# q·k as three fp32r products in row tiles of 32, in place of six bf16 products in row tiles of 64

## The chip, the cores and the metric

One core of one Trainium2 chip. The metric is the device time of one execution in microseconds (us).

## What is computed

The reference, cut to what matters here (4 batches of 1024 tokens, width 128, 16 heads of width 8, 8 experts of which a router weighs the best two for each token):

```python
xn  = layernorm(x)                                   # (4, 1024, 128), fp32
zn  = layernorm(xn) * ln_w + ln_b
q, k, v = split(zn @ W_qkv + b_qkv)                  # each (4, 16, 1024, 8)
scores = einsum('bhqd,bhkd->bhqk', q, k) / sqrt(8)   # the products that the change is about
attn = softmax(scores);  msa = attn @ v
s = xn + msa @ W_proj + b_proj
ffn = sum over e of weight[e] * (gelu(xn @ W1[e] + b1[e]) @ W2[e] + b2[e])
result = x + s * silu(ffn)
```

## The kernel before

The results must be nearly as exact as fp32. Matmuls get there in three ways: fp32 operands as they are (each then has two records in the profile), operands split into two fp32r parts and multiplied in three products (most of the experts), and, for q and k, operands split into three bf16 parts and multiplied in six products.

**The rows of q and k.** The 4096 tokens are worked through in 8 groups g of 512. For each, q and k (w = 0 and 1) come transposed into `qk_full`. VectorE casts them to the first bf16 part (`first`, L1153), GpSimd subtracts that part (`rest`, L547), VectorE casts the second (`second`, L1159), and GpSimd makes the third (`third`, L554). These four steps stand in slots 20 to 26 of a group's 32. SyncE then stores the parts in HBM (`sp_store_qk`, L398 to L405) so that each of a head's 8 dimensions has six slots, with the parts of q and of k in such an order that slot times slot gives the six products. A head so has 48 rows, and one matmul with 48 contraction rows sums all six products over all dimensions. In the stacks for the scores three more rows hold the negative maximum of each query: 51 rows.

**Two heads at a time.** There are 32 pairs p of heads. A pair is loaded (`sp_rows`, L424) into slot p % 2 of a stack: its first head at partitions 0 and up, its second at 64 and up (`HALF`). Matmuls whose rows lie in different halves run side by side in TensorE's array, those in the same half one after the other. `q_max_stack` and `k_max_stack` serve the maxima (L867), `q_stack` and `k_stack` the scores that are exponentiated (L927).

**The expert phase** takes the first 523 us or so. TensorE goes through 32 slots for each group, most with three fp32r matmuls up (L832, L833, L834) and three down (L853, L854, L856; each fourth one is in fp32, L848). Beside them, 128 early maximum steps (`early_scores`, at `EARLY_AT`) cover head pairs 0 to 7: each is two matmuls of L867, one for each head, which VectorE reduces in one instruction (L1237). GpSimd and VectorE split the experts' hidden values (`h_lo`, L612 and L1181), and SyncE's queue, worked off in program order, loads each group's tokens `xz` (L381), for which VectorE's L1079 waits.

**The attention phase** has 256 blocks n of 128 keys of a pair p = n // 8. Each has two halves of 512 queries. A half is two matmuls of L927 (one for each head), which fill one of two PSUM buffers, and one ACTIVATE of 128x1024 on ScalarE (L753), the exponential. Beside the scores of blocks 0 to 239 TensorE computes the maxima of later pairs (L867, pairs 8 to 31), 3.2 matmuls a block, each into one of three PSUM banks and reduced by its own VectorE instruction (L1219); their pair is p' = 8 + n // 10. The order on TensorE in a half is: scores of one head, maximum of the other head, scores of the other head, and mostly a maximum of the first. The scores of a half wait until the exponential of the half before the last is done. After a block's two halves come the 8 records (4 matmuls) of attn @ v (L947) of the block before the last, and now and then transposes (L901 of the maxima, L960 of the output). Engines wait for each other by semaphores, and every engine works in program order.

Of the kernel before, what the change touches and what calls it, by code (L numbers as in the profile page):

```python
# [5 lines left out]
ALU = mybir.AluOpType  # L6
# [7 lines left out]
P = 128  # L14
TG = 512
TT = TG // P
PARTS = 3
SLOTS = 6
Q_PARTS = (0, 1, 2, 0, 1, 0)
K_PARTS = (0, 1, 0, 1, 0, 2)  # L20
HALF = 64
# [33 lines left out]
def attention_and_experts(nc, x, ln_w, ln_b, w_qkv, b_qkv, w_proj, b_proj, w1, b1, w2, b2, w_r, b_r, out):  # L55
# [25 lines left out]
    assert D == P and N % TG == 0 and N // TG == 2 and HID % P == 0 and SROWS <= HALF  # L81
# [5 lines left out]

    q_dram = nc.dram_tensor("q_rows_dram", (B, D, SLOTS, N), BF16, kind="Internal").ap()
    k_dram = nc.dram_tensor("k_rows_dram", (B, D, SLOTS, N), BF16, kind="Internal").ap()
    w_dram = nc.dram_tensor("expert_w_dram", (NG, TT, E, P), F32, kind="Internal").ap()  # L90
    m_dram = nc.dram_tensor("neg_max_dram", (PAIRS, NM, P), BF16, kind="Internal").ap()

    with ExitStack() as ctx:
# [11 lines left out]
        q_s = sb("q_stack", [P, 2, N], BF16)  # L105
        k_s = sb("k_stack", [P, 2, N], BF16)
        q_m = sb("q_max_stack", [P, 2, N], BF16)
        k_m = sb("k_max_stack", [P, 2, N], BF16)
        ident = sb("ident", [P, P])
        ident_b = sb("ident_b", [P, P], BF16)  # L110
# [3 lines left out]
        nmp = sb("neg_max_parts", [P, 2, 2, PARTS, NT], BF16)  # L114
        nmT = sb("neg_max_t", [NM, 2, P], BF16)
# [19 lines left out]
        qkp = fs("qk_parts", [P, 2, PARTS, TG], BF16)  # L135
# [162 lines left out]

        def split(i):

            return i % HC < SC
# [61 lines left out]
        QP_ST = 6 * 16  # L363
# [25 lines left out]
        def sp_store_qk(sp, g):  # L389
# [13 lines left out]
            sp.dma_start(dst[:, 0:2, :], qkp[:, 1, 0:2, :]).then_inc(S("qp_st"), 16)  # L403
            sp.dma_start(dst[:, 2:4, :], qkp[:, 1, 0:2, :]).then_inc(S("qp_st"), 16)
            sp.dma_start(dst[:, 4:6, :], qkp[:, 1, 0:3:2, :]).then_inc(S("qp_st"), 16)  # L405
# [25 lines left out]
        def sp_load_max(sp, p):  # L431
# [3 lines left out]
            for hh in range(2):  # L435
                sp.dma_start(q_s[HALF * hh + QROWS:HALF * hh + SROWS, slot, :],
# [920 lines left out]
```

## Time and profile before

| | us |
|---|---|
| median of three runs (1129.59 to 1134.57) | 1129.85 |
| the profiled execution's own time | 1131.14 |
| its span, from first to last instruction | 1129.3 |

| engine | busy us | share of the span |
|---|---|---|
| TensorE matmuls | 1062.4 | 94% |
| TensorE weight loads | 438.8 | 39% |
| VectorE | 896.3 | 79% |
| ScalarE | 847.7 | 75% |
| GpSimd | 365.0 | 32% |

A matmul's record lasts from its start until its result has drained, so that records of matmuls that follow each other overlap: the distance of two starts says how long a matmul holds the array, not the duration of its record. The mean granted TensorE clock was 0.988 of full speed.

### The profile page before, as it was taken

The page shows a single profiled execution, that of the slowest core. Times are in us where ns is not written, and L with a number is a line of the kernel's source. Part 1 is how long each engine was busy: PE and PEld are TensorE (multiplying, and loading weights), DVE is VectorE, ACT ScalarE, POOL GpSimd, SP SyncE. Part 2 cuts the span into 40 slices and gives each one's busy share as a digit, 9 for nine tenths or more (in the row PEclk, how much of TensorE's full clock was granted, in tenths as well). Part 3 has the DMA queues.
Part 4 walks back from the last instruction along what each step waited for, and adds up shares of the span by engine and source line. Part 5 has one row for each costly group of instructions (what it writes and reads, how often), then busy time and mean ns, then how long its engine had stood idle before and what let it go on. Part 6 is the DMA issues. An engine that isn't in the chain of part 4 may idle for free.

```text
span 1129.3 us, 17260 instructions
## 1 busy us (share of the span) xinstructions
PE 1062.4 (94%) x6041; PEld 438.8 (39%) x6041; DVE 896.3 (79%) x1567; ACT 847.7 (75%) x1133; POOL 365.0 (32%) x534
## 2 busy tenths in 40 slices
PE   5698999999999999999999999999999999999995
PEld 4475656566666666663122222222121212212123
DVE  7566778777768687666999999999999999999715
ACT  6575666566666666667988898888889898988982
POOL 3795656656666666453010001000000000000001
PEclk9899999999999999998999999999999999999998
DMA  4523131414141322223111112111211111111102
GB/s 144 150 83 84 61 86 29 117 34 118 32 114 33 102 51 64 75 72 92 45 44 44 39 35 56 32 45 29 58 31 44 40 48 45 30 44 30 30 1 75
DMA packets 84992, 67.42 MB, mean 60 GB/s; under 512 B 9277, under 2 KB 71402, under 8 KB 84906
## 3 DMA queue, kind: packets, MB, share of 16 engines
q1 hardware_dynamic: 84906, 66.32, 21.7%
q8 instruction: 48, 0.79, 0.3%
q14 instruction: 38, 0.31, 0.1%
HBM read 51.08 MB, written 15.20 MB: 59 GB/s over the span
## 4 chain that ended last, share of the span: by engine, by line
PE 53%; ACT 19%; DVE 6%; issue 4%; ACTq 0%; DVEq 0%; POOL 0%; POOLq 0%
ACT p_ring L753 17%; PE psum L947 13%; PE psum L927 11%; PE psum L867 6%; PE psum L832 4%; PE psum L848 3%; PE psum L834 3%; PE psum L833 3%; PE psum L856 2%; PE psum L853 2%; PE psum L854 2%; DVE neg_max_half L1237 2%; PE psum L960 2%; DVE neg_max_half L1219 1%; PE psum L981 1%
## 5 line engine op out<-in xcount | busy, mean ns | idle before, releaser
L753 ACT ACTIVATE p_ring<-psum 128x1024 f32<-128x1024 f32 x512 | 500.7, 1023 | 66.0 <-PE psum L927 62.3
L1219 DVE TENSOR_REDUCE neg_max_half<-psum 128x1 f32<-128x512 f32 x768 | 486.3, 684 | 38.1 <-PE psum L867 29.0
L867 PE MATMUL psum<-k_max_stack,q_max_stack 48*128 48x512 bf16 x1024 | 300.6, 386 | 15.7 <-DVE neg_max_half L1237 9.6
L927 PE MATMUL psum<-q_stack,k_stack 51*128 51x512 bf16 x1024 | 279.1, 383 | 12.9 <-ACT p_ring L753 3.7
L947 PE MATMUL psum<-p_ring,v_sb 128*9 128x512 f32 x2048 | 268.5, 597 | 0.4 <-ACT o_sb L744 0.4
L716 ACT ACTIVATE h_hi<-psum,cols 128x512 fp32r<-128x512 f32 x192 | 132.0, 688 | 152.1 <-PE psum L834 147.9
L612 POOL TENSOR_TENSOR h_lo<-h_split,h_hi 128x512 fp32r<-128x512 f32 x128 | 164.5, 1289 | 141.0 <-ACT h_split L719 139.2
L1237 DVE TENSOR_REDUCE neg_max_half<-psum 128x2 f32<-128x1024 f32 x128 | 156.5, 1222 | 60.6 <-PE psum L867 60.4
L927 PEld LDWEIGHTS psum<-q_stack,k_stack 51*128 51x128 bf16 x1024 | 60.3, 94 | 305.8 <-ACT p_ring L753 281.4
L568 POOL CAST neg_max_parts<-neg_max_rest 128x16 bf16<-128x16 f32 x32 | 6.7, 211 | 510.6 <-DVE neg_max_rest L1228 510.6
L719 ACT ACTIVATE h_split<-psum,cols 128x512 f32<-128x512 f32 x192 | 130.9, 682 | 0.0
L832 PE MATMUL psum<-xn_t_hi,w_hi 128*128 128x512 f32 x256 | 128.4, 502 | 1.2 <-DVE w_lo L292 1.2
L867 PEld LDWEIGHTS psum<-k_max_stack,q_max_stack 48*128 48x128 bf16 x1024 | 69.6, 93 | 116.6 <-issue 43.3
L834 PE MATMUL psum<-xn_t_lo,w_hi 128*128 128x512 f32 x256 | 102.1, 399 | 0.0
L833 PE MATMUL psum<-xn_t_hi,w_lo 128*128 128x512 f32 x256 | 101.7, 397 | 0.0
L1181 DVE TENSOR_TENSOR h_lo<-h_split,h_hi 128x512 fp32r<-128x512 f32 x64 | 53.7, 839 | 50.8 <-ACT h_split L719 50.8
L856 PE MATMUL psum<-h_lo,w_hi 128*128 128x512 f32 x192 | 77.2, 402 | 9.1 <-POOL h_lo L612 4.6
L853 PE MATMUL psum<-h_hi,w_hi 128*128 128x512 f32 x192 | 76.4, 398 | 0.0
L854 PE MATMUL psum<-h_hi,w_lo 128*128 128x512 f32 x192 | 76.0, 396 | 0.0
L603 POOL TENSOR_TENSOR acc<-acc,prod 128x512 f32<-128x512 f32 x48 | 65.8, 1371 | 15.0 <-DVE prod L1198 15.0
L947 PEld LDWEIGHTS psum<-p_ring,v_sb 128*9 128x9 f32 x2048 | 31.0, 88 | 92.4 <-issue 92.1
L848 PE MATMUL psum<-h_full,w_full 128*128 128x512 f32 x128 | 65.4, 592 | 0.0
(114 smaller groups left out, 920.4 us busy)
## 6 DMA issues: line engine op xcount, KB each, us to landing
expert_w_bc<-expert_w_dram SPq DMA_DIRECT2D x64, 256.0 KB, 4.9
k_rows_dram<-qk_parts SPq DMA_DIRECT2D x24, 256.0 KB, 3.0
q_max_stack<-q_rows_dram SPq DMA_DIRECT2D x64, 96.0 KB, 2.5
k_max_stack<-k_rows_dram SPq DMA_DIRECT2D x64, 96.0 KB, 2.5
q_stack<-q_rows_dram SPq DMA_DIRECT2D x64, 96.0 KB, 2.5
k_stack<-k_rows_dram SPq DMA_DIRECT2D x64, 96.0 KB, 2.5
q_rows_dram<-qk_parts SPq DMA_DIRECT2D x8, 384.0 KB, 2.6
xz<-in_L_attn_z_dram SPq DMA_DIRECT2D x8, 256.0 KB, 3.2
```

The lines of the kernel that those rows point to most:

```text
L612: pool.tensor_tensor(hl[:, (g * HS + j) % HR, :], h32[:, (g * HS + j) % FR, :], hh[:, (g * HS + j) % HR, :].bitcast(F32), ALU.subtract)\
L716: act.activation(hh[:, (g * HS + j) % HR, :], up, ACT.Gelu, bias=col(C_B1 + i))\
L719: act.activation(h32[:, (g * HS + j) % FR, :], up, ACT.Gelu, bias=col(C_B1 + i))\
L753: act.activation(p_sb[:, n % PR, a, :, :].rearrange("p h t -> p (h t)"), scores_bank[s % 2], ACT.Exp, scale=SCALE).then_inc(S("P"), 1)
L832: pe.matmul(o, w1h[:, e, ws], G(xh, g), start=True, stop=False)
L833: pe.matmul(o, w1l[:, e, ws], G(xh, g), start=False, stop=False)
L834: pe.matmul(o, w1h[:, e, ws], G(xl, g), start=False, stop=True).then_inc(S("h"), 1)
L867: return pe.matmul(to, q_m[rows, slot, t * P:(t + 1) * P], k_m[rows, slot, c * TG:(c + 1) * TG], start=True, stop=True)
L927: i = pe.matmul(scores_bank[s % 2][:, hh * TG:(hh + 1) * TG], k_s[rows, slot, kt * P:(kt + 1) * P], q_s[rows, slot, a * TG:(a + 1) * TG], ...
L947: i = pe.matmul(o_bank[at:at + VR, :], v_sb[:, b * KT + kt, 2 * (p % PB) + hh, :], p_sb[:, n % PR, a, hh, :], start=(kt == 0), stop=(kt == ...
L1219: dve.tensor_reduce(mx[:, p % MXR, c, hh * NT + t:hh * NT + t + 1], ring_bank(("max", u)), AX.X, ALU.max, negate=True).then_inc(S("R"), 1)
L1237: dve.tensor_reduce(mx[:, p % MXR, c, :].rearrange("p (h t) -> p h t", h=2)[:, :, t], early_bank, AX.X, ALU.max, negate=True).then_inc(S(" ...
```

## The change

q and k are split into two fp32r parts (`PARTS` = 2), whose three products fill three slots (`SLOTS` = 3): a head has 24 rows, 26 with the parts of its maximum. Each head takes a row tile of 32 partitions: pairs with even p the tiles at partitions 0 and 32, pairs with odd p those at 64 and 96, so that the stacks need no second slot. VectorE's second cast is gone, and GpSimd makes the second part in one step. Of the maximum's parts GpSimd makes two in two steps, not three in four. The stores are four instead of six for a group. The numbers of matmuls, reductions and exponentials stay the same.

```diff
-PARTS = 3
-SLOTS = 6
-HALF = 64
+PARTS = 2
+SLOTS = 3
+ROWS = 32
...
-        q_s = sb("q_stack", [P, 2, N], BF16)
-        k_s = sb("k_stack", [P, 2, N], BF16)
+        q_s = sb("q_stack", [P, N])
+        k_s = sb("k_stack", [P, N])
...
+        def tile_row(p, hh):
+
+            return ROWS * (2 * (p % 2) + hh)
...
-            sp.dma_start(dst[:, 0:3, :], qkp[:, 0, :, :]).then_inc(S("qp_st"), 16)
-            sp.dma_start(dst[:, 3:5, :], qkp[:, 0, 0:2, :]).then_inc(S("qp_st"), 16)
-            sp.dma_start(dst[:, 5:6, :], qkp[:, 0, 0:1, :]).then_inc(S("qp_st"), 16)
+            sp.dma_start(dst[:, 0:2, :], qkp[:, 0, :, :].bitcast(F32)).then_inc(S("qp_st"), 16)
+            sp.dma_start(dst[:, 2:3, :], qkp[:, 0, 0:1, :].bitcast(F32)).then_inc(S("qp_st"), 16)
...
-                        pool.tensor_tensor(qkf[:, w, :], qkf[:, w, :], qkp[:, w, 0, :], ALU.subtract)\
-                            .then_inc(S("r1"), 1)
-                    return step
-
-                def third(w):
-                    def step():
-                        wait(pool, "p1", g, 2, w + 1)
-                        pool.tensor_tensor(qkp[:, w, 2, :], qkf[:, w, :], qkp[:, w, 1, :], ALU.subtract)\
+                        pool.tensor_tensor(qkp[:, w, 1, :], qkf[:, w, :], qkp[:, w, 0, :].bitcast(F32), ALU.subtract)\
                             .then_inc(S("qp"), 1)
...
-                slot = p % 2
-                rows = slice(HALF * hh, HALF * hh + QROWS)
-                return pe.matmul(to, q_m[rows, slot, t * P:(t + 1) * P], k_m[rows, slot, c * TG:(c + 1) * TG],
+                rows = slice(tile_row(p, hh), tile_row(p, hh) + QROWS)
+                return pe.matmul(to, q_m[rows, t * P:(t + 1) * P].bitcast(F32R),
+                                 k_m[rows, c * TG:(c + 1) * TG].bitcast(F32R),
                                  start=True, stop=True)
...
-                def second(w):
-                    def step():
-                        wait(dve, "r1", g, 2, w + 1)
-                        dve.tensor_copy(qkp[:, w, 1, :], qkf[:, w, :]).then_inc(S("p1"), 1)
-                    return step
...
-                        20: [first(0)], 21: [first(1)], 24: [second(0)], 25: [second(1)], 28: [values]}
+                        20: [first(0)], 21: [first(1)], 28: [values]}
```

TensorE's program keeps its order. On GpSimd, this stood at the splitting of group 1 before (L547 and L554 split q and k, L612 splits the experts' hidden values, L603 adds up the experts):

```order
L547 TENSOR_TENSOR qk_full<-qk_full,qk_parts 128x512
L612 TENSOR_TENSOR h_lo<-h_split,h_hi 128x512
L603 TENSOR_TENSOR acc<-acc,prod 128x512
L554 TENSOR_TENSOR qk_parts<-qk_full,qk_parts 128x512
L612 TENSOR_TENSOR h_lo<-h_split,h_hi 128x512
L554 TENSOR_TENSOR qk_parts<-qk_full,qk_parts 128x512
```

And this stands there now, from the same place on (its L547, L600 and L591 are the former L554, L612 and L603):

```order
L547 TENSOR_TENSOR qk_parts<-qk_full,qk_parts 128x512
L600 TENSOR_TENSOR h_lo<-h_split,h_hi 128x512
L591 TENSOR_TENSOR acc<-acc,prod 128x512
L600 TENSOR_TENSOR h_lo<-h_split,h_hi 128x512 x2
L591 TENSOR_TENSOR acc<-acc,prod 128x512
```

The parts of k are complete two instructions of GpSimd's own splitting earlier, ahead of one addition and one or two steps of the experts. Behind them SyncE stores the parts, loads the stacks of pairs 0 and 1 and then `xz`.

## Rows read from the trace of the kernel before

**Rows 1.** Busy us (xcount) of each engine in stretches, clock, DMA:

```profile
200.00:300.00 100.00, 94.94 (x399) 60.50 (x397) 75.49 (x128) 60.88 (x105) 63.17 (x95) 1.00 0.30 78
832.87:923.92 91.05, 88.57 (x636) 18.60 (x632) 84.19 (x148) 80.73 (x91) 3.31 (x16) 1.00 0.15 41
923.92:1014.97 91.05, 88.57 (x636) 18.61 (x632) 84.20 (x148) 80.73 (x91) 3.31 (x16) 1.00 0.15 41
```

**Rows 2.** Groups by form: busy us, mean ns of one, idle before:

```profile
L753 ACT ACTIVATE p_ring<-psum 128x1024 f32<-128x1024 f32 x512 | 500.7, 1023 | 66.0 <-PE psum L927 62.3
L1219 DVE TENSOR_REDUCE neg_max_half<-psum 128x1 f32<-128x512 f32 x768 | 486.3, 684 | 38.1 <-PE psum L867 29.0
L1237 DVE TENSOR_REDUCE neg_max_half<-psum 128x2 f32<-128x1024 f32 x128 | 156.5, 1222 | 60.6 <-PE psum L867 60.4
```

**Rows 3.** Timeline, expert phase: start us, duration us; matmuls, then weight loads:

```profile
299.61 0.40 PE L856 MATMUL psum<-h_lo,w_hi 128*128 128x512 f32 x1
299.94 0.39 PE L867 MATMUL psum<-k_max_stack,q_max_stack 48*128 48x512 bf16 x2
300.26 0.50 PE L832 MATMUL psum<-xn_t_hi,w_hi 128*128 128x512 f32 x1
300.60 0.39 PE L833 MATMUL psum<-xn_t_hi,w_lo 128*128 128x512 f32 x1
300.83 0.39 PE L834 MATMUL psum<-xn_t_lo,w_hi 128*128 128x512 f32 x1
...
299.94 0.10 PEld L867 LDWEIGHTS psum<-k_max_stack,q_max_stack 48*128 48x128 bf16 x2 [0.36 <-issue]
300.26 0.19 PEld L832 LDWEIGHTS psum<-xn_t_hi,w_hi 128*128 128x128 f32 x1 [0.23 <-issue]
300.37 0.19 PEld L833 LDWEIGHTS psum<-xn_t_hi,w_lo 128*128 128x128 f32 x1
```

**Rows 4.** Timeline, attention phase: exponentials, matmuls, weight loads:

```profile
844.26 3.88 ACT L753 ACTIVATE p_ring<-psum 128x1024 f32<-128x1024 f32 x4 [0.98 <-PE psum L927]
848.47 1.02 ACT L753 ACTIVATE p_ring<-psum 128x1024 f32<-128x1024 f32 x1 [0.33 <-PE psum L927]
...
846.79 1.04 PE L947 MATMUL psum<-p_ring,v_sb 128*9 128x512 f32 x8
847.77 0.39 PE L927 MATMUL psum<-q_stack,k_stack 51*128 51x512 bf16 x1
848.00 0.59 PE L927 MATMUL psum<-q_stack,k_stack 51*128 51x512 bf16 x2
...
846.25 0.09 PEld L927 LDWEIGHTS psum<-q_stack,k_stack 51*128 51x128 bf16 x1 [0.63 <-ACT p_ring L753]
847.76 0.09 PEld L927 LDWEIGHTS psum<-q_stack,k_stack 51*128 51x128 bf16 x1 [0.86 <-ACT p_ring L753]
847.77 0.11 PEld L867 LDWEIGHTS psum<-k_max_stack,q_max_stack 48*128 48x128 bf16 x2
847.78 0.10 PEld L927 LDWEIGHTS psum<-q_stack,k_stack 51*128 51x128 bf16 x1
```

**Rows 5.** Timeline, last blocks, which have no maxima beside them:

```profile
1083.99 0.39 PE L927 MATMUL psum<-q_stack,k_stack 51*128 51x512 bf16 x2 [0.27 <-ACT p_ring L753]
1084.31 1.04 PE L947 MATMUL psum<-p_ring,v_sb 128*9 128x512 f32 x8
...
1086.13 5.75 ACT L753 ACTIVATE p_ring<-psum 128x1024 f32<-128x1024 f32 x6
```

**Rows 6.** Timeline, group 1's parts of k and group 2's tokens:

```profile
69.38 1.34 POOL L547 TENSOR_TENSOR qk_full<-qk_full,qk_parts 128x512 f32<-128x512 f32 x1
76.19 1.17 POOL L554 TENSOR_TENSOR qk_parts<-qk_full,qk_parts 128x512 bf16<-128x512 f32 x1
77.38 0.54 SPq L403 DMA_DIRECT2D k_rows_dram<-qk_parts  x1
86.02 0.42 SPq L381 DMA_DIRECT2D xz<-in_L_attn_z_dram  x1
...
89.29 0.29 DVE L1079 BATCH_NORM_STATS2 bn_parts<-xz 128x6 f32<-128x128 f32 x1 [7.80 <-DMA xz<-in_L_attn_z_dram]
...
90.23 0.50 PE L856 MATMUL psum<-h_lo,w_hi 128*128 128x512 f32 x1 [2.55 <-DVE h_lo L1181]
92.33 0.63 PE L854 MATMUL psum<-h_hi,w_lo 128*128 128x512 f32 x1
```

More of the change, by code:

```diff
@@ L80, in attention_and_experts @@
     NM = 2 * PARTS * NT
[L81 removed]
+    assert D == P and N % TG == 0 and N // TG == 2 and HID % P == 0 and SROWS <= ROWS
     x_g = x.rearrange("b (g t p) d -> (b g) p t d", p=P, t=TT)
     out_g = out.rearrange("b (g t p) d -> (b g) p t d", p=P, t=TT)
[L88 to L89 removed]
+    q_dram = nc.dram_tensor("q_rows_dram", (B, D, SLOTS, N), F32, kind="Internal").ap()
+    k_dram = nc.dram_tensor("k_rows_dram", (B, D, SLOTS, N), F32, kind="Internal").ap()
     w_dram = nc.dram_tensor("expert_w_dram", (NG, TT, E, P), F32, kind="Internal").ap()
[L91 removed]
+    m_dram = nc.dram_tensor("neg_max_dram", (PAIRS, NM, P), F32, kind="Internal").ap()
     with ExitStack() as ctx:
@@ L535, in _ @@
         def _(pool):
-            for n, t in enumerate((ident, ident_b)):
-                pool.memset(t[:, :], 0.0).then_inc(S("pool"), 1)
-                pool.wait_ge(S("pool"), n + 1)
-                pool.affine_select(out=t[:, :], in_=t[:, :], compare_op=ALU.not_equal, fill=1.0, base=0,
-                                   pattern=[[-1, P]], channel_multiplier=1).then_inc(S("ident"), 1)
+            pool.memset(ident[:, :], 0.0).then_inc(S("pool"), 1)
+            pool.wait_ge(S("pool"), 1)
+            pool.affine_select(out=ident[:, :], in_=ident[:, :], compare_op=ALU.not_equal, fill=1.0, base=0,
+                               pattern=[[-1, P]], channel_multiplier=1).then_inc(S("ident"), 1)
             ch = Chain(pool, S("pool_own"))
@@ L622, in padding @@
             def padding():
-                pool.memset(k_s[:, :, :], 1.0).then_inc(S("ones"), 1)
+                pool.memset(k_s[:, :], 1.0).then_inc(S("ones"), 1)
                 pool.memset(v_sb[:, :, :, DH:VR], 1.0).then_inc(S("v_ones"), 1)
@@ L724, in neg_max_t @@
             def neg_max_t(p, early=False):
-                m_tr = (b5 if early else ring_bank(("mT", p)))[0:NM, 0:P // 2].bitcast(BF16)
+                m_tr = (b5 if early else ring_bank(("mT", p)))[0:NM, 0:P]
                 act.wait_ge(S("mT"), p + 1)
@@ L767, in _ @@
         def _(pe):
-            pe.wait_ge(S("ident"), 2)
+            pe.wait_ge(S("ident"), 1)
             pe.wait_ge(S("rows"), 6 * 16)
@@ L899, in m_t @@
                     ring_free(pe, ("mT", p))
-                m_tr = (b5 if early else ring_bank(("mT", p)))[0:NM, 0:P // 2].bitcast(BF16)
-                pe.transpose(m_tr, nmp[:, p % 2, :, :, :].rearrange("p h i t -> p (h i t)"), ident_b[:, :])\
+                m_tr = (b5 if early else ring_bank(("mT", p)))[0:NM, 0:P]
+                pe.transpose(m_tr, nmp[:, p % 2, :, :, :].rearrange("p h i t -> p (h i t)").bitcast(F32), ident[:, :])\
                     .then_inc(S("mT"), 1)
@@ L925, in scores @@
                 for k, hh in enumerate((first, 1 - first)):
-                    rows = slice(HALF * hh, HALF * hh + SROWS)
-                    i = pe.matmul(scores_bank[s % 2][:, hh * TG:(hh + 1) * TG], k_s[rows, slot, kt * P:(kt + 1) * P],
-                                  q_s[rows, slot, a * TG:(a + 1) * TG], start=True, stop=True)
+                    rows = slice(tile_row(p, hh), tile_row(p, hh) + SROWS)
+                    i = pe.matmul(scores_bank[s % 2][:, hh * TG:(hh + 1) * TG], k_s[rows, kt * P:(kt + 1) * P].bitcast(F32R),
+                                  q_s[rows, a * TG:(a + 1) * TG].bitcast(F32R), start=True, stop=True)
                     if k:
```

35 lines of the change are left out of this document (14 added, 21 removed).

## The prediction

> **What bounds the kernel now.** I read the busy times by stretch first. In the expert phase TensorE is busy for 94.94 of 100 us and every other engine for at most 75.49 [rows 1], so what TensorE's program gains or loses there, the kernel does. In the attention phase the stretches repeat exactly: 91.05 us each, with 636 matmul records [rows 1]. A block has 8 + 4 + 3.2 = 15.2 records, and 40 blocks with their 28 transposes make 636, so a stretch is 40 blocks and a block takes 2.28 us. VectorE is busy for 84.19/40 = 2.10 us of it and ScalarE for 80.73/40 = 2.02 us. None of the engines is full: they wait for each other. The groups say the same, with 66.0 us in which ScalarE idles before its exponentials, nearly all for L927, and 38.1 us in which VectorE idles before its single reductions [rows 2].
>
> The timeline shows the loop that sets the pace of an undisturbed stretch. Four exponentials start at 844.26, the next at 848.47, 0.33 us after ScalarE fell idle [rows 4]: 4.21 us for two blocks. Two exponentials of that stretch must end before the scores whose weights load at 846.25 may start. From there TensorE is without a break on the path: scores and maxima, attn @ v at 846.79, scores again at 847.77, the second head's at 848.00, whose end frees the exponential at 848.47 [rows 4]. The remaining 0.17 us a block (2.28 less 2.11) comes from transposes and from maxima that wait for a PSUM bank. So half of the loop is TensorE's, and its matmuls count in both phases.
>
> **What the change costs on TensorE.** The rate of streaming hardly changes. Full-array fp32r matmuls start 0.23 us apart (300.60 to 300.83) [rows 3], and bf16 score pairs 847.77 to 848.00, also 0.23 [rows 4]. I take 0.01 us more for each step of two.
>
> The weights are dearer. A bf16 load of 128 columns lasts 0.10 us, an fp32r one 0.19, and the next fp32r load starts 0.11 us after it (300.26, 300.37) [rows 3]. Behind running matmuls that is hidden: L833 starts at 300.60, long after its load, and its record lasts the usual 0.39. Where the array changes its tiling, it isn't: L832 behind the maximum pair lasts 0.50 instead of 0.39, and its successor starts 0.34 us later instead of 0.23. The bf16 pair at the same kind of place lasts 0.39 with its load exposed [rows 3]. An exposed fp32r load thus costs 0.10 us more than a bf16 one. No row shows fp32r weights in a row tile; the bounds are 0 (the load hides in the change of tiling) and 0.19 (the whole record). I take 0.10, since the fp32r row beside it is the same load at the same kind of place.
>
> The Trainium skill, TensorE: Matmul & The Clock Gate, section Weight-path perf modes, says that the fast weight load works for 128 columns of any type but fp32. The trace agrees (0.10 against 0.19 us). By that page's rates, 128/1.2 ns against a quarter of it, an exposed load would cost an estimated 0.08 us more, and the expert term below would be 12 instead of 15 us.
>
> Expert phase: 128 maximum pairs (L1237 has 128 instances [rows 2]), each with an exposed load and a slower step, 0.10 + 0.017 = 0.118 us by L832's 0.34 and the 0.23 spacing: **+15.1 us**. Nothing hides it, as TensorE is full there. Bounds 0 and 128 x 0.23 = 29.
>
> Attention, blocks where p and p' = 8 + n // 10 have the same parity (120 of the 240 with maxima, counted from the order of the blocks): scores and maxima lie in the same two tiles, so pairs run one after the other as now. The loop of two blocks crosses two exposed loads, at 846.25 after the wait and at 847.77 after attn @ v, and about five steps: 2 x 0.10 + 0.05 = 0.25 us, 0.125 a block. Part of the blocks are held by VectorE's banks and transposes instead, so I take 0.10: **+12 us**. Bounds 0 and 0.20 (three exposed loads, as with a transpose): 0 to +24.
>
> The other 120 blocks: scores and maxima lie in four different tiles. Then the two pairs of a half need not follow each other, which saves 0.23 us a half and leaves 0.125 to pay: 0.23 x 2 - 0.25 = 0.21 us off the loop of two blocks, if only two of its four steps lie on the path. All four (both halves of both blocks) would save more. That such halves work is shown by the last blocks, whose halves are one pair: scores 1083.99, attn @ v 1084.31, and six exponentials in 5.75 us, back to back [rows 5], so 1.9 us a block. With maxima, VectorE's 2.10 us is the floor, 0.18 below the present 2.28. I take 0.14, between the loop's 0.10 and the floor's 0.18 and nearer to that, because disturbed blocks gain too: **-17 us**, bounds 0 and -21.
>
> Whether loads into different tiles overlap is decided by one row: the score load starts at 847.76, two maximum loads and the second score load start from 847.77 to 847.78, and each lasts 0.09 [rows 4]. Two heads load at once.
>
> The 16 last blocks have the two exposed loads and little else: 16 x 0.10 = **+2 us**.
>
> **What it saves elsewhere.** VectorE's 16 casts and half of GpSimd's splitting lie beside a full TensorE, and cost or save nothing, except in group 1. There the last part of k ends at 76.19 + 1.17, SyncE stores it at 77.38, goes through eight loads and issues `xz` only at 86.02; VectorE waits for it for 7.80 us and TensorE for 2.55 us in turn [rows 6]. In the new order the part of k is ready when L547 at 69.38 ends, 70.7, 6.6 us earlier, and one store is gone. `xz` lands around 82, and TensorE's wait goes: -2.6. After this wait the granted clock was at its lower level (1.2 GHz) for some matmuls: L854 at 92.33 lasts 0.63 instead of 0.39 [rows 6]. I count eight matmuls with 0.2 us each that come back: -1.6. GpSimd's other backlogs, about 0.8. Together **-5 us**; if the clock falls anyway, -3. The maximum's parts, two steps fewer of GpSimd, stand in the shadow of later pairs. The stacks' loads have the same bytes, and whole blocks of time before they are needed.
>
> Sum: 15.1 + 12 - 17 + 2 - 5 = +7.1. The profiled execution took 1131.14, 1.3 above the median of the runs, so 1138.2 in its terms and **1137 us** against 1129.85: 0.6% slower.
>
> **The rivals.**
>
> *Four tiles pay in full, loads hide* (faster, 1115). The unlike blocks come down to VectorE's floor, -21; the like ones wait for VectorE so often that only +5 shows; in the expert phase the load is prefetched while the array changes its tiling, so that 128 x 0.017 = +2 is left: 1129.85 + 2 + 5 - 21 + 1 - 5 = 1112, or 1115 with a little of the exposure. For it: the 38.1 us of VectorE's waits [rows 2]. Against it: L832's 0.50 [rows 3]. It decides once an exposed load costs under 0.03 us. Chance 0.22.
>
> *Two of four tiles only* (slower, 1167). Scores and maxima of unlike pairs still run two at a time. Then all 240 blocks pay 0.10: 15 + 24 + 2 - 5 = +36, 1166. Against it: nothing but that no row has four tiles of rows; for it: the same. Chance 0.14. The Trainium skill, same page, section Part 3: Packing small matmuls, has four row tiles running at once; no row here shows that.
>
> *Loads into the same rows wait for the matmul* (slower, about 1163). Each second pair of a half in like blocks then shows its load of 0.11: 120 x 2 x 0.11 = +26 on 1137. L833's load, hidden in the same rows [rows 3], speaks against it. Chance 0.03. The Trainium skill, same section, states just that rule, that weights load beside a running matmul only in other row groups; the trace disagrees for the whole array, so the sum goes without it.
>
> *Tiles of fp32r load one after the other* (slower, about 1210). Each second load of 0.11 is exposed: 128 x 0.11 = +14 more in the expert phase, 2 x 0.11 a block in 240 blocks = +53 more. Against it the overlapping bf16 loads [rows 4], of which none is fp32r. Chance 0.08.
>
> **How the numbers follow.** Forecast 0.53, with its own range from 1126 to 1149 by the bounds of the two attention terms. The range for all goes from 1115, the faster rival's time, to 1168, above the two-tile rival: left out are the last rival and the outer half of the first. About 0.5% (5.6 us) is what can be told from no change: 1124.2 to 1135.5. Slower: 0.33 of the forecast's 0.53 and the three slow rivals, 0.25, make 0.58. Same: 0.16 of the forecast and 0.04 of the faster rival, 0.20. Faster: the rest, 0.22.
>
> **What would show it.** L867 in the expert phase lasts about 0.49 and its successor starts 0.42 instead of 0.32 us after it. The first L832 or L853 behind it is unchanged. In attention, stretches of like parity take over 2.3 us a block, those of unlike parity about 2.15, with four matmuls starting together. `xz` of group 2 lands before 84 us and no clock dip follows. The prediction is wrong if unlike blocks don't beat like ones by 0.15 us or more, or if the expert phase ends at the same time as before.

## The result: 3.4% slower, outside the range

| kernel | median us | lowest to highest | ratio to before |
|---|---|---|---|
| before | 1130.17 | 1129.59 to 1134.57 | |
| changed | 1181.53 | 1168.93 to 1204.09 | 1.0343 [1.0307, 1.0379] |
| changed, second measurement | 1180.97 | 1169.62 to 1204.55 | 1.0357 [1.0337, 1.0378] |

The ratios leave out those executions of the changed kernel, about half, that took 1190 us and more: in the profiled one TensorE's clock fell a second time, between 1082.8 and 1137.4 us; the others took 1169 to 1172 us, and the profile read here is of one of these (1169.62). Forecast was 1137 in a range from 1115 to 1168. So the sign was right, the size was 32 us short, and the range ended 1 to 4 us below those times.

The groups of the second measurement, by form (busy us, mean ns of one, idle before and its releaser), answer to [rows 2]:

```profile
L741 ACT ACTIVATE p_ring<-psum 128x1024 f32<-128x1024 f32 x512 | 496.5, 1024 | 98.6 <-PE psum L915 97.4
L1201 DVE TENSOR_REDUCE neg_max_half<-psum 128x1 f32<-128x512 f32 x768 | 484.7, 685 | 70.5 <-PE psum L854 66.7
L854 PE MATMUL psum<-k_max_stack,q_max_stack 24*128 24x512 f32 x1024 | 351.6, 484 | 23.1 <-DVE neg_max_half L1219 12.6 <-DVE neg_max_half L1201 8.1
L854 PEld LDWEIGHTS psum<-k_max_stack,q_max_stack 24*128 24x128 f32 x1024 | 142.1, 185 | 109.6 <-issue 42.9 <-DVE neg_max_half L1219 31.5 <-DVE neg_max_half L1201 29.0
```

Neither ScalarE nor VectorE has more work than before; both wait longer for TensorE, ScalarE 98.6 us instead of 66.0 and VectorE 70.5 instead of 38.1. The weight load of a maximum takes 185 ns. (L741, L854, L915, L935, L1201 and L1219 are the former L753, L867, L927, L947, L1219 and L1237; L820 to L822, L844, L382 and L1067 are the former L832 to L834, L856, L381 and L1079.)

The windows show where the time lies: the expert phase, the head of attention, the 17 us behind it, and blocks 16 to 55 and 56 to 95.

```profile
200.00:300.00 100.00, 95.98 (x392) 62.03 (x391) 73.06 (x125) 60.91 (x105) 57.18 (x85) 1.00 0.23 58
528.00:558.70 30.70, 30.37 (x125) 10.86 (x129) 18.27 (x30) 16.03 (x18) 0.30 (x1) 0.50 0.30 86
558.70:575.45 16.75, 16.75 (x112) 6.10 (x104) 14.64 (x28) 13.76 (x16) 1.66 (x3) 1.00 0.14 39
575.45:667.95 92.50, 87.39 (x636) 28.08 (x632) 83.66 (x148) 79.44 (x89) 6.61 (x12) 1.00 0.15 41
667.95:764.29 96.34, 94.37 (x635) 32.59 (x632) 84.05 (x148) 80.88 (x89) 4.14 (x10) 1.00 0.14 39
```

The same 40 blocks took 91.05 us before [rows 1]. Now they take 92.50 where 8 of them are like and 32 unlike, and 96.34 where 32 are like ("like" means that scores and maxima have pairs of the same parity, so that they share two tiles). The second row was not in any term of the forecast: for 30.70 us TensorE is busy nearly all the time at a clock of 0.50, with 18 instructions of ScalarE in it; before, 30 ran in such a stretch. Before, the kernel had the lower clock for 6.80 us at the same place:

```profile
521.70:528.50 6.80, 6.80 (x28) 1.22 (x31) 5.43 (x10) 4.81 (x6) 0.00 (x0) 0.50 1.00 266
528.50:559.20 30.70, 29.80 (x218) 6.07 (x210) 28.01 (x48) 26.88 (x30) 2.07 (x5) 1.00 0.14 41
```

The starts of the exponentials cut the whole time. In us, from the profiles, before and changed:

| part | before | changed | difference | forecast |
|---|---|---|---|---|
| to the first exponential (517.99, 526.13) | 518.0 | 526.1 | +8.1 | +10.1 |
| blocks 0 to 15 (14 like) | 38.9 | 49.3 | +10.5 | +1.1 |
| blocks 16 to 223, like (92) | 209.6 | 221.4 | +11.8 | +9.2 |
| blocks 16 to 223, unlike (116) | 264.2 | 268.3 | +4.2 | -16.4 |
| block 224 to the last exponential, 16 blocks with maxima (14 like) and 16 without | 67.4 | 71.5 | +4.2 | +3.1 |
| end | | | -0.3 | 0 |
| span | 1129.3 | 1167.7 | +38.4 | +7.1 |

The forecast's column spreads its two attention terms evenly over the blocks they were meant for (+12 us over 120 like blocks, -17 over 120 unlike ones). Two cells hold most of the 31 us that are missing: the unlike blocks (21) and the head of attention (9).

### The profile page after: what moved, and what is told of

It reads as the page before. It is cut to its first block, busy times and chain, and to the rows that moved or that the text cites. A ratio compares the mean times of both kernels' runs of the same rounds, so it can differ in the third digit from the quotient of the medians.

```text
span 1189.7 us, 17145 instructions
## 1 busy us (share of the span) xinstructions
PE 1120.5 (94%) x6041; PEld 533.0 (45%) x6041; DVE 887.0 (75%) x1551; ACT 844.8 (71%) x1133; POOL 331.5 (28%) x452
## 4 chain that ended last, share of the span: by engine, by line
PE 64%; ACT 8%; DVE 8%; issue 3%; ACTq 0%; DVEq 0%; POOL 0%; POOLq 0%
PE psum L935 18%; PE psum L915 16%; PE psum L854 8%; ACT p_ring L741 7%; PE psum L820 4%; DVE neg_max_half L1201 4%; PE psum L836 3%; PE psum L822 3%; PE psum L821 3%; PE psum L841 2%; PE psum L842 2%; PE psum L844 2%; DVE neg_max_half L1219 2%; PE psum L948 1%; PE psum L969 1%
## 5 line engine op out<-in xcount | busy, mean ns | idle before, releaser
L741 ACT ACTIVATE p_ring<-psum 128x1024 f32<-128x1024 f32 x512 | 496.7, 1024 | 117.4 <-PE psum L915 116.4
L1201 DVE TENSOR_REDUCE neg_max_half<-psum 128x1 f32<-128x512 f32 x768 | 484.5, 684 | 82.4 <-PE psum L854 78.4
L854 PE MATMUL psum<-k_max_stack,q_max_stack 24*128 24x512 f32 x1024 | 356.7, 490 | 22.9 <-DVE neg_max_half L1219 12.4
L915 PE MATMUL psum<-q_stack,k_stack 26*128 26x512 f32 x1024 | 294.7, 479 | 10.8 <-ACT p_ring L741 10.6
L935 PE MATMUL psum<-p_ring,v_sb 128*9 128x512 f32 x2048 | 285.6, 632 | 0.9
L915 PEld LDWEIGHTS psum<-q_stack,k_stack 26*128 26x128 f32 x1024 | 128.8, 193 | 296.8 <-ACT p_ring L741 262.4
L600 POOL TENSOR_TENSOR h_lo<-h_split,h_hi 128x512 fp32r<-128x512 f32 x128 | 164.3, 1287 | 174.4 <-ACT h_split L707 173.2
L1219 DVE TENSOR_REDUCE neg_max_half<-psum 128x2 f32<-128x1024 f32 x128 | 156.4, 1222 | 73.6 <-PE psum L854 73.0
L854 PEld LDWEIGHTS psum<-k_max_stack,q_max_stack 24*128 24x128 f32 x1024 | 144.8, 188 | 110.0 <-issue 43.0
L560 POOL CAST neg_max_parts<-neg_max_rest 128x16 fp32r<-128x16 f32 x32 | 6.9, 215 | 565.1 <-DVE neg_max_rest L1210 564.9
L820 PE MATMUL psum<-xn_t_hi,w_hi 128*128 128x512 f32 x256 | 129.2, 505 | 1.2 <-DVE w_lo L289 1.2
L821 PE MATMUL psum<-xn_t_hi,w_lo 128*128 128x512 f32 x256 | 102.2, 399 | 0.0
L822 PE MATMUL psum<-xn_t_lo,w_hi 128*128 128x512 f32 x256 | 102.1, 399 | 0.0
L844 PE MATMUL psum<-h_lo,w_hi 128*128 128x512 f32 x192 | 76.0, 396 | 4.7 <-POOL h_lo L600 3.2
L591 POOL TENSOR_TENSOR acc<-acc,prod 128x512 f32<-128x512 f32 x48 | 65.2, 1358 | 19.3 <-DVE prod L1180 19.2
L935 PEld LDWEIGHTS psum<-p_ring,v_sb 128*9 128x9 f32 x2048 | 31.2, 89 | 82.7 <-issue 70.7
```

Source lines behind the costliest of these rows:

```text
L600: pool.tensor_tensor(hl[:, (g * HS + j) % HR, :], h32[:, (g * HS + j) % FR, :], hh[:, (g * HS + j) % HR, :].bitcast(F32), ALU.subtract)\
L741: act.activation(p_sb[:, n % PR, a, :, :].rearrange("p h t -> p (h t)"), scores_bank[s % 2], ACT.Exp, scale=SCALE).then_inc(S("P"), 1)
L820: pe.matmul(o, w1h[:, e, ws], G(xh, g), start=True, stop=False)
L821: pe.matmul(o, w1l[:, e, ws], G(xh, g), start=False, stop=False)
L822: pe.matmul(o, w1h[:, e, ws], G(xl, g), start=False, stop=True).then_inc(S("h"), 1)
L854: return pe.matmul(to, q_m[rows, t * P:(t + 1) * P].bitcast(F32R), k_m[rows, c * TG:(c + 1) * TG].bitcast(F32R), start=True, stop=True)
```

## The experiments

Theory after the result: an exposed fp32r load costs what was forecast, four tiles give back less than forecast, and the head of attention is slow because TensorE's clock stays at its lower level while only two tiles of 24 to 26 rows are at work. Rivals: VectorE's reductions eat what four tiles give; the fp32r products themselves keep the clock down.

**0. The changed kernel once more,** unedited.

> The changed kernel once more, to have a profile of its undisturbed executions. Theory of the loads and the clock: against before +9 us at the end of the expert phase (128 pairs, 0.11 us each, less the 5 of group 2's tokens), +20 in blocks 16 to 224 and their like (94.4 us instead of 91.05 for 40 blocks), +10 from the lower clock in the first eight blocks: 1169. Rival, that only the clock makes the difference and the blocks' own cost is an effect of the disturbed execution: 40 blocks take 91 us here and the whole is near 1145.

Measured: the second measurement of the table above, 1169.62 in the profiled execution, as the theory had it. The groups and windows above are its own. The rival, 91 us for 40 blocks, is out: they take 92.50 and 96.34 at the full clock.

**1. The changed kernel with bf16 parts** separates the type from the tiles. It carries two bf16 parts instead of two fp32r ones, which hold fewer bits, in the same rows and tiles.

```diff
-        q_s = sb("q_stack", [P, N])
+        q_s = sb("q_stack", [P, N], BF16)
...
-        qkp = fs("qk_parts", [P, 2, PARTS, TG], F32R)
+        qkp = fs("qk_parts", [P, 2, PARTS, TG], BF16)
```

> The changed kernel with q and k in two bf16 parts: 24 and 26 bf16 rows in the same tiles of 32. The products are then only those of two bf16 parts, less exact. Theory of the loads: bf16 loads cost next to nothing where they are exposed, so blocks of like parity take 2.28 us as before, those of unlike parity gain up to 0.17, and the expert phase ends 5 us sooner than before: 1110 to 1120, and 1130 if the clock stays low at the start of attention for tiles of few rows. Rival, that tiles of 32 rows themselves cost (change of tiling, or four tiles sharing something): about as slow as the changed kernel, 1155 or more.

Measured: 1119.1 (1118.3 to 1119.3), 0.9900 [0.9885, 0.9914]. The first exponential starts at 511.80, 14.3 us earlier than with fp32r and 6.2 earlier than before. A like block takes 2.250 us, an unlike one 2.188. So what fp32r loads cost in blocks 16 to 223 is 0.156 for a like and 0.125 for an unlike block, and four tiles with bf16 loads give only 0.09 against the kernel before. The rival, that the tiles themselves cost (1155 or more), is out. The clock still stays down for 27.30 us at the head of attention, with bf16 operands: it isn't fp32r that keeps it there. With the clock down, 1130 had been expected; the time was 11 us better than that.

```profile
515.00:542.30 27.30, 27.30 (x122) 4.14 (x124) 16.81 (x28) 16.00 (x17) 0.00 (x0) 0.50 0.30 82
542.30:572.00 29.70, 28.16 (x208) 6.10 (x200) 27.73 (x51) 26.04 (x31) 3.31 (x6) 1.00 0.08 22
```

**2. The kernel before with `xz` of group 2 ahead of group 1's stores** tests the saving.

```diff
+                if g == 1:
+                    sp_load_x(sp, 2)
...
-                if g + 1 < NG:
+                if 1 < g < NG - 1:
```

> The kernel before, with the load of group 2's tokens ahead of group 1's stores on SyncE's queue, and nothing else. My term for this effect was -5: -2.6 of TensorE's wait and -1.6 of the lower clock after it, here without the 0.8 of GpSimd's backlog: 1126. Rival: the wait is only moved to the next late thing, less than 1 us gained: 1129 to 1130.

Measured: 1127.3 (1126.3 to 1128.7), 0.9973 [0.9963, 0.9983]; in the profiles the first exponential is 3.4 us earlier. The wait and the clock dip behind it, forecast at 4.2, are over half of the 6.2 us that experiment 1 gained ahead of attention.

**3. Always four tiles.** Scores have the two lower tiles and maxima the two upper ones for every pair; two slots again, and `q_m`, `k_m` are the same tensors as `q_s`, `k_s`, so that they fit.

```diff
-        q_s = sb("q_stack", [P, N])
+        q_s = sb("q_stack", [P, 2, N])
+        q_m = q_s
...
-            return ROWS * (2 * (p % 2) + hh)
+            return ROWS * (2 * top + hh)
```

> The changed kernel with the scores always in the lower two tiles and the maxima always in the upper two (two slots in the free dimension of one shared stack), so that every block is one of unlike parity. Theory of the loads and the clock: the 120 like blocks lose their extra 0.09 us against unlike ones, -11, and the clock rises at once at the start of attention, -8: 1150. Rival, that four tiles at once give nothing and the differences between the blocks come from their numbers of maxima: same as the changed kernel, 1169.

Measured: 1143.2 (1142.3 to 1143.4), 1.0111 [1.0094, 1.0128]. That is 7 us better than expected. All blocks are now alike, 2.28 us on average, as long as before the change: the exposed loads and the four tiles cancel. And the clock is back after 6.80 us. This is the head of attention and blocks 16 to 55:

```profile
530.40:537.20 6.80, 6.60 (x30) 2.40 (x28) 5.25 (x10) 4.07 (x5) 0.00 (x0) 0.50 1.01 296
537.20:567.90 30.70, 28.67 (x217) 8.62 (x214) 28.34 (x49) 26.82 (x30) 1.65 (x3) 1.00 0.17 46
566.28:657.50 91.22, 84.81 (x635) 26.34 (x632) 83.31 (x148) 79.25 (x89) 6.59 (x12) 1.00 0.15 40
```

**4 and 5. Half of each single reduction left out** (256 of 512 keys are searched for the maximum), in the changed kernel and in the one before.

```diff
-... ring_bank(("max", u)), AX.X, ALU.max,
+... ring_bank(("max", u))[:, 0:TG // 2], AX.X, ALU.max,
```

> The changed kernel with VectorE's single reductions over the first 256 keys of each bank only (the maximum subtracted in the softmax is then one over half of the keys). Blocks 16 to 223. Theory that the loop of VectorE and TensorE over three PSUM banks, with its exposed fp32r loads, took the unlike blocks' gain: with reductions 0.27 us shorter, unlike blocks fall from 2.31 to about 2.0 us (my loop of two blocks, 4.0 us) and like ones to 2.2 to 2.25. Rival, that four fp32r tiles at once are held up by TensorE or ScalarE in some other way: unlike blocks stay above 2.2.

> The kernel before with the same shorter reductions. Blocks 16 to 223. By the loop of two blocks read in my prediction (4.21 us), 2.11 to 2.15 us a block instead of 2.28, the same for like and unlike ones. Then the exposed loads show as 0.1 us between this kernel's like blocks and those of the changed one. Rival, that transposes and not banks make up the rest: 2.2 or more.

Measured, one execution each: 1159.7 and 1117.8. In the changed kernel a like block falls from 2.406 to 2.336 and an unlike one from 2.313 to 2.223, in the kernel before both from 2.278 to about 2.22. So VectorE holds 0.06 of a block before and 0.09 of an unlike block after: part of what four tiles should have given, not all of it. Both theories missed (about 2.0 for an unlike block, 2.11 to 2.15 before the change) and both rivals, 2.2 and more, came out; the exposed loads showed as forecast, 0.117 between the like blocks of the two. The gain sits in the blocks with four maxima, those whose n is a multiple of 5: the shorter reductions take them from 2.57 to 2.31 us before the change and from 2.79 to 2.49 after it, and save 0.01 and 0.03 in the others.

In the changed kernel this execution also kept the lower clock for 61.4 us at the head of attention, twice as long as in experiment 0, so that its 1159.7 can't be set against 1117.8; the lower clock reaches into blocks 16 and 17, and without these two an unlike block takes 2.21 us:

```profile
527.40:588.70 61.30, 60.67 (x255) 19.51 (x255) 22.23 (x57) 33.96 (x37) 1.64 (x3) 0.50 0.19 54
```

**6 and 7. Two bf16 parts at partitions 0 and 64,** so that never more than two tiles are at work, without and with rows of zeros up to 48 and 51 rows. The two differ in nothing else but the writing of the zeros when the kernel starts.

```diff
-            return ROWS * (2 * (p % 2) + hh)
+            return 64 * hh
```

```diff
+                for z in (q_s, q_m, k_m):
+                    pool.memset(z[:, :, :], 0.0).then_inc(S("ones"), 1)
...
-                rows = slice(tile_row(p, hh), tile_row(p, hh) + QROWS)
+                rows = slice(tile_row(p, hh), tile_row(p, hh) + 48)
...
-                    rows = slice(tile_row(p, hh), tile_row(p, hh) + SROWS)
+                    rows = slice(tile_row(p, hh), tile_row(p, hh) + 51)
```

> 24 and 26 bf16 rows as in c_bf16_rows32, but both pairs' heads at partitions 0 and 64 as in the kernel before, with two slots: never more than two tiles at once. Theory that the clock stays at its lower level in attention while only two tiles of some 25 rows work at a time: it has no unlike blocks that could end this, so the clock is low for far longer than 27 us and the time is well above 1160. Rival, that the clock comes back after 27 to 31 us by itself whatever runs: 2.28 us a block, 1130 to 1136.

> The same, with rows of zeros up to the 48 and 51 rows of the kernel before, in both products. The array's timing is that of the kernel before. Theory that the number of rows at work decides the clock: as in the kernel before, low for some 7 us at the start of attention, 1122 to 1126. If rows of zeros don't count as work: as c64_bf16_two_tiles. Rival that the clock has nothing to do with rows: both kernels the same.

Measured: 1253.0 to 1500.1 (median 1410.6) without the zeros, 1129.3 (1128.4 to 1129.8) with them. The windows of the fastest execution without zeros, and of the one with them:

```profile
515.10:836.00 320.90, 320.90 (x1317) 54.46 (x1316) 179.12 (x306) 172.17 (x187) 11.85 (x23) 0.50 0.07 18
836.00:1152.50 316.50, 307.36 (x2199) 64.03 (x2198) 292.25 (x513) 279.62 (x309) 5.79 (x28) 1.00 0.08 22
```

```profile
519.00:525.80 6.80, 6.54 (x27) 1.18 (x27) 5.11 (x10) 3.88 (x4) 0.00 (x0) 0.50 0.98 278
525.80:836.00 310.20, 301.71 (x2157) 63.02 (x2153) 287.19 (x499) 275.51 (x304) 13.97 (x33) 1.00 0.08 22
```

TensorE is busy for 320.90 of 320.90 us at the lower clock, and ScalarE gets through 187 instructions, where 304 run with the zeros. With rows of zeros the same instructions run at the full clock after 6.80 us, and the kernel is as fast as before the change. A time of 1122 to 1126 had been expected: the first exponential starts at 516.50 instead of 511.78, since GpSimd first writes the zeros and TensorE's first wait for VectorE grows from 3.8 to 8.6 us. Without the zeros the clock is back at 836 and then stays up for 316.50 us with the same two tiles of few rows. Four full-array transposes (L950, 835.12 to 835.81) stand just before its return; nine such groups since 558.07 had not brought it back.

**8. The changed kernel with rows of zeros up to 32** (each tile full).

```diff
-                rows = slice(tile_row(p, hh), tile_row(p, hh) + QROWS)
+                rows = slice(tile_row(p, hh), tile_row(p, hh) + ROWS)
```

> The changed kernel with rows of zeros behind the 24 or 26, so that each product has 32 rows in its tile (two tiles then hold 64 rows instead of 48 to 52). Instructions, loads, places and lengths are the same. Theory one, the rows that two tiles have at work decide the clock at the head of attention: the 30.7 us at the lower clock behind 528.0 shrink, to 7 us as in the kernel before if 64 rows are enough, and the time goes from 1170 to 1160. Theory two, it is the fp32r products or chance that keep the clock down there: 1169 to 1171 as without the zeros. Rows of zeros that cost time of their own would show in the blocks behind 560 us: over 2.41 us in a block of like parity.

Measured: 1170.0 (1168.8 to 1170.1), 1.0340 [1.0325, 1.0356]. The time is that of theory two; its fp32r products are excluded by experiment 1, chance isn't. The 7 us of theory one missed: the lower clock lasts 27.30 us, against 30.70:

```profile
530.80:558.10 27.30, 27.13 (x112) 9.43 (x111) 16.11 (x27) 14.73 (x16) 0.00 (x0) 0.50 0.32 92
```

Two tiles with 64 rows in all had the lower clock for 27.30 us here, two with 96 to 102 for 6.80 (experiment 7), and so had four with 100 (experiment 3). Blocks of like parity take 2.404 us with the zeros and 2.406 without: the rows of zeros cost no time in the products.

**9. Maxima from the upper 16 bits.** As experiment 3, but the maxima are products of the upper halves of the fp32r rows, read as bf16. They are coarser, the scores aren't.

```diff
-                return pe.matmul(to, q_m[rows, p % 2, t * P:(t + 1) * P].bitcast(F32R),
+                return pe.matmul(to, q_m[rows, p % 2, t * P:(t + 1) * P].bitcast(BF16)[:, 1::2],
```

> As the kernel in which scores always have the lower two tiles and maxima the upper two (1143), but the maxima are products of the upper 16 bits of the same fp32r rows, read as bf16 with a stride; the scores are fp32r as before. The maxima are thus coarser, the scores not. Theory one, what an exposed fp32r load costs: the 128 pairs of the expert phase fall back from 430 to about 320 ns (-13), and in attention, where a maximum that waited for its bank shows its load again, -0.02 a block (-5): 1125. Rival, the strided reads load slowly or stream at half the rate: no gain in the expert phase and 0.23 more where two maxima stream, 1143 or more, up to 1200.

Measured: 1118.6 (1118.0 to 1123.5), 0.9898 [0.9874, 0.9922]. The first exponential starts at 509.87, 18.2 us earlier than in experiment 3, and a block takes 2.250 instead of 2.283. 13 us there and 1125 in all had been expected. The loads explain 128 x 0.11 = 14 of the 18.2; experiment 3 also has two stretches of 3.4 us at the lower clock (from 253.9 and 448.5) that this kernel lacks. The strided reads cost nothing that these numbers show. TensorE's timeline around an early maximum, first of the changed kernel (matmuls, then their loads), then of this one:

```profile
298.69 0.39 PE L844 MATMUL psum<-h_lo,w_hi 128*128 128x512 f32 x1
299.01 0.50 PE L854 MATMUL psum<-k_max_stack,q_max_stack 24*128 24x512 f32 x2
299.44 0.50 PE L820 MATMUL psum<-xn_t_hi,w_hi 128*128 128x512 f32 x1
299.78 0.40 PE L821 MATMUL psum<-xn_t_hi,w_lo 128*128 128x512 f32 x1
300.02 0.40 PE L822 MATMUL psum<-xn_t_lo,w_hi 128*128 128x512 f32 x1
...
299.01 0.18 PEld L854 LDWEIGHTS psum<-k_max_stack,q_max_stack 24*128 24x128 f32 x2 [0.35 <-issue]
...
299.78 0.19 PEld L822 LDWEIGHTS psum<-xn_t_lo,w_hi 128*128 128x128 f32 x1
```

```profile
296.43 0.40 PE L844 MATMUL psum<-h_lo,w_hi 128*128 128x512 f32 x1
296.76 0.40 PE L854 MATMUL psum<-k_stack,q_stack 24*128 24x512 bf16 x2
297.08 0.50 PE L820 MATMUL psum<-xn_t_hi,w_hi 128*128 128x512 f32 x1
...
296.75 0.10 PEld L854 LDWEIGHTS psum<-k_stack,q_stack 24*128 24x128 bf16 x2 [0.36 <-issue]
```

From the pair's start to its successor's it is 0.43 us with fp32r loads and 0.32 with bf16 loads (0.32 before, too [rows 3]).

**10. Two bf16 parts and always four tiles,** experiments 1 and 3 together.

> Two bf16 parts (less exact than the fp32r ones), scores always in the lower two tiles of 32 rows and maxima in the upper two. If gains add up, the version with bf16 parts in tiles by parity (1119.1) loses its blocks of like parity (2.250 down to 2.19, 92 blocks and the first 16: -6) and most of its 27.3 us at the lower clock (-7): 1106. Rival: in these blocks VectorE and the transposes set the pace, as the half-size reductions suggest, and the clock stays low for other reasons: 1115 to 1119.

Measured: 1096.9 (1096.9 to 1099.2), 0.9704 [0.9686, 0.9721], 9 us better than the gains added up. The lower clock lasts 6.80 us (1 had 27.30), and a block takes 2.164 us in either parity.

```profile
514.70:521.50 6.80, 6.54 (x32) 1.00 (x36) 5.53 (x10) 4.60 (x5) 0.00 (x0) 0.50 1.04 285
548.21:634.68 86.47, 76.67 (x635) 17.26 (x633) 82.64 (x148) 78.93 (x89) 6.58 (x12) 1.00 0.08 22
```

**11. The same with half of each single reduction left out,** the edit of experiments 4 and 5.

> The kernel with two bf16 parts and always four tiles, in which VectorE's single reductions read 256 of the 512 keys (it leaves out half of the search for the maximum, VectorE is busy about 0.5 us less in a block). Theory one, VectorE's share of the loop is what is left of a block with four tiles: 2.164 us falls by 0.15 or more, to about 2.0, which is what ScalarE is busy, and the time from 1096.9 to 1062. Rival, it is ScalarE's four exponentials in a block and the scores behind them, as in the kernel before and in the changed one, where the same edit gave 0.06 and 0.09 a block: 2.164 falls by 0.05 to 0.09, 1078 to 1087.

Measured, one execution: 1072.1. A block falls by 0.10 to 2.06 us, of which ScalarE is busy for 1.96. The rival had 0.05 to 0.09 and theory one 0.15 or more; block and time both lie between and nearer the rival. With four tiles and cheap loads VectorE is worth more than before, and of what is then left ScalarE is busy for 95%:

```profile
545.80:628.10 82.30, 74.52 (x636) 16.14 (x636) 51.53 (x148) 78.28 (x89) 6.55 (x12) 1.00 0.09 24
```

## Why the prediction was wrong

**Right: the price of an exposed fp32r load in the expert phase.** "0.10 + 0.017 = 0.118 us" a pair; the pair's spacing grew by 0.11, and 15.1 us were forecast against 14.3 (changed kernel against experiment 1) and 18.2 us (experiment 3 against 9, with two clock dips in it). The 0.017 in that sum has no row behind it; the 0.01 taken for a slower step doesn't give it.

**Right: the saving.** 5 us forecast, 6.2 measured ahead of attention (experiment 1 against before), 3.4 of them by `xz` alone (experiment 2). In the changed kernel `xz` is issued early, and VectorE waits for it for 1.29 us instead of 7.80 [rows 6]; TensorE's clock doesn't dip behind it:

```profile
77.47 0.40 SPq L382 DMA_DIRECT2D xz<-in_L_attn_z_dram  x1
81.82 0.29 DVE L1067 BATCH_NORM_STATS2 bn_parts<-xz 128x6 f32<-128x128 f32 x1 [1.29 <-DMA xz<-in_L_attn_z_dram]
```

**Right: four tiles work at once, and so do their loads.** The timeline of a half in an unlike block of the changed kernel, two scores and two maxima:

```profile
766.28 0.18 PEld L915 LDWEIGHTS psum<-q_stack,k_stack 26*128 26x128 f32 x1 [0.64 <-ACT p_ring L741]
766.28 0.50 PE L915 MATMUL psum<-q_stack,k_stack 26*128 26x512 f32 x1 [0.33 <-ACT p_ring L741]
766.29 0.18 PEld L854 LDWEIGHTS psum<-k_max_stack,q_max_stack 24*128 24x128 f32 x1
766.29 0.49 PE L854 MATMUL psum<-k_max_stack,q_max_stack 24*128 24x512 f32 x1
```

The second score and maximum start at 766.29 as well. That settles two rivals: tiles that pay two at a time (1167, near the measured time, but for another reason) and fp32r loads one after the other (called 1210, though its own terms, 14 and 53 on 1137, make 1204). By the Trainium skill, TensorE: Matmul & The Clock Gate, Part 3: Packing small matmuls, four row tiles run concurrently; the trace agrees, to within 0.01 us. That section's rule, that a load overlaps running matmuls only in other rows, the trace of the changed kernel contradicts again (experiment 9's first timeline): the load of L822 starts at 299.78, together with L821's matmul in the same rows, and lasts 0.19, and L822 starts at 300.02, 0.24 us behind L821.

**Nearly right: the like blocks.** 0.10 forecast, 0.128 measured, inside its bounds. The loads alone cost more than assumed (0.156 against 0.125, experiment 1); like blocks with bf16 parts take 0.028 less than before the change, for which no run shows a reason.

**The step that failed first: the unlike blocks.** "I take 0.14, between the loop's 0.10 and the floor's 0.18 and nearer to that, because disturbed blocks gain too." They lose. The load's part of the sum held (0.125 assumed, 0.125 measured, experiment 1 against the changed kernel). The gain of four tiles had to be 0.265 (0.14 and the loads' 0.125) and measured 0.09. Us a block, means of blocks 16 to 223:

| unlike blocks | before | bf16 parts (1) | changed |
|---|---|---|---|
| n a multiple of 5, with four maxima (23) | 2.581 | 2.585 | 2.817 |
| the others (93) | 2.202 | 2.090 | 2.188 |

In the first row the maximum waits for its PSUM bank, which VectorE frees. There four tiles save nothing, and behind the wait the fp32r load is exposed once more: blocks 195, 200 and 205 take 2.47, 2.54 and 3.07 before, 2.46, 2.54 and 3.07 with bf16 parts, and 2.69, 2.76 and 3.29 in the changed kernel, 0.22 more each. In the second row four tiles save 0.11 and the loads take 0.10 of it back. Single pairs of blocks there behave as worked out: 1.95 + 2.26 = 4.21 us before, 1.86 + 2.18 = 4.04 after (blocks 202, 203), so -0.09 a block against the -0.10 of the loop; the 93 on average gain 0.014. Why they save 0.11 and not 0.23 is not shown. With bf16 parts and without transposes they take 2.035 us, which leaves little above the 1.9 us of exponentials back to back [rows 5]: ScalarE, not VectorE's 2.10, may be the floor there. Block 195 in the changed kernel, and then with bf16 parts:

```profile
997.20 0.50 PE L915 MATMUL psum<-q_stack,k_stack 26*128 26x512 f32 x1 [0.26 <-ACT p_ring L741]
...
997.72 0.18 PEld L854 LDWEIGHTS psum<-k_max_stack,q_max_stack 24*128 24x128 f32 x1 [0.33 <-DVE neg_max_half L1201]
997.72 0.50 PE L854 MATMUL psum<-k_max_stack,q_max_stack 24*128 24x512 f32 x1
998.15 0.12 PEld L935 LDWEIGHTS psum<-p_ring,v_sb 128*9 128x9 f32 x8 [0.25 <-ACT p_ring L741]
...
999.76 1.02 ACT L741 ACTIVATE p_ring<-psum 128x1024 f32<-128x1024 f32 x1 [0.75 <-PE psum L915]
```

```profile
954.87 0.39 PE L917 MATMUL psum<-q_stack,k_stack 26*128 26x512 bf16 x1 [0.37 <-ACT p_ring L743]
...
955.28 0.09 PEld L856 LDWEIGHTS psum<-k_max_stack,q_max_stack 24*128 24x128 bf16 x1 [0.32 <-DVE neg_max_half L1203]
955.28 0.38 PE L856 MATMUL psum<-k_max_stack,q_max_stack 24*128 24x512 bf16 x1
955.60 0.12 PEld L937 LDWEIGHTS psum<-p_ring,v_sb 128*9 128x9 f32 x8 [0.23 <-issue]
...
957.10 1.02 ACT L743 ACTIVATE p_ring<-psum 128x1024 f32<-128x1024 f32 x1 [0.45 <-PE psum L917]
```

The maximum holds up attn @ v for 0.43 us instead of 0.32 (997.72 to 998.15, 955.28 to 955.60), and ScalarE idles for 0.75 instead of 0.45. That VectorE's banks are part of the limit, experiments 4 and 5 show (0.09 and 0.06 a block, most of it in blocks with four maxima). In experiments 10 and 11 the part is 0.10.

A sign of being wrong that the prediction named came true: unlike blocks had to beat like ones by 0.15 us or more, and they do so by 0.093. And the forecast's own range, 1126 to 1149, isn't what the bounds of its two attention terms give: 0 to +24 and 0 to -21, around the other terms, make 1121 to 1166. The measured 1169 to 1172 lies above these too; the clock, next, was in none of the terms.

**The step that was missing: the clock at the head of attention.** The forecast took every block at the full clock; blocks 0 to 15 lost 10.5 us where 1.1 were forecast. Experiments 6 and 7 show that the rows decide: rows of zeros alone, with the same instructions, turn 320.9 us at the lower clock (1.2 GHz) into 6.8. It isn't the type of the operands (27.3 us with bf16, experiment 1), nor how long TensorE is busy (all of the 320.9 us). The first eight blocks are like, with two tiles of 24 to 26 rows. The changed kernel's first unlike block begins at 555.3, and its clock is back at 558.7; with bf16 parts these are 539.1 and 542.3. With four tiles from the start it is back after 6.8 us (experiments 3, 9, 10). But the first unlike block doesn't end it each time: in experiment 4 blocks 8 and 9, unlike too, passed at the lower clock (552.0 to 558.4), and it was back only at 588.7, among the next unlike ones (16 and 17). Nor do few rows bring the clock down wherever they stand: 32 like blocks of 56 to 95 ran at the full clock, and so did experiment 6 from 836 on. What the runs show is that the clock, once down at the head of attention, comes back late while two tiles of few rows are at work; when it does is open. The clock's second fall (54.6 us in the profile of the first measurement) also lies in blocks nearly all with two tiles at work, 7 of the last 16 among them; that this is the same mechanism is likely and wasn't tried:

```profile
1082.80:1137.40 54.60, 54.60 (x213) 16.19 (x213) 18.56 (x34) 30.04 (x34) 0.42 (x2) 0.50 0.06 16
```

The Trainium skill, TensorE: Matmul & The Clock Gate, Part 1: The HAM clock gate, has the clock follow how busy TensorE is; these traces disagree in that busy time with few rows didn't bring the full clock back.

**Experiment 3 adds up the two.** It takes 26 us less than the changed kernel's profile in experiment 0: 11 in blocks 0 to 15, 15 in blocks 16 to 223, 2.5 behind them, less 2 ahead of attention. Of the 13 us that it still takes over the kernel before, 10 lie ahead of the first exponential, since a block takes 2.28 us in both.

**The rival that came nearest in time** was "two of four tiles only", 1167 against 1169 to 1172. Its mechanism is wrong: four tiles do run, and the number came near by luck. It has unlike blocks pay 0.10 each, 11.6 us for the 116 of blocks 16 to 223, where 4.2 were measured; the lower clock of the head, 9 us that it doesn't have, fills the place.

**What stays open.** When the clock comes back with few rows, and why four tiles save 0.11 in the other unlike blocks. Why experiment 10 is 9 us better than the sum of its gains: about 5 us of that lie in blocks 16 to 223, whose unlike blocks take 2.163 us instead of the 2.188 of experiment 1, perhaps because a like block leaves its neighbours a backlog of banks; this is only argued.

## What to carry to other kernels

Count a gain that comes from overlap only in those iterations in which the overlapped pair really is on the path: here a look at single blocks of the kernel before (1.95 and 2.26, but 2.47 to 3.07 each fifth, with a wait for VectorE in it) would have said that each fifth gains nothing. When an edit makes products smaller in contraction rows, look at what it does to the clock, and try rows of zeros. In the products they took no time here (2.404 against 2.406 us a block); writing them when the kernel starts did (4.7 us in experiment 7). An fp32r operand is priced by its exposed loads, at each change of tiling and behind each wait; reading the upper halves of the same rows as bf16 removes the price where coarse products do.

## What the runs showed of the hardware

- TensorE, busy for 320.90 of 320.90 us with bf16 products of 24 and 26 rows in two tiles, kept a granted clock of 0.50 all that time; its mean over an execution was 0.865 in the fastest and 0.688 in the slowest (1500 us). With rows of zeros up to 48 and 51 it was at 1.00 after 6.80 us: rows of zeros count. Up to 32 rows in each of two tiles they changed little (27.30 instead of 30.70 us), and four tiles of 24 and 26 rows did as well as two of 48 and 51 (6.80). Once up, the clock stayed at 1.00 for 316.50 us with the same two tiles of 24 and 26 rows.
- Weight loads into different row tiles overlap, fp32r as well as bf16 (0.18 us each, starts within 0.01 us).
- A strided bf16 read of the upper halves of fp32 rows loads in 0.10 us, like packed bf16, and its matmul streams no slower (0.40).
